# Residual, normalising, modulating and gating of token rows moved from VectorE to GpSimd inside a causal attention stage

## The reference, cut to what matters

```
mod = silu(c) @ wmod                  # sa, ca, ga, sb, cb, gb: six rows of 256 per sequence
ga, gb = clipped away from zero       # |g| >= 0.25
h = layernorm(x) * (1 + ca) + sa
x = x + ga * attention(h)             # 16 heads of 16 features, causal, full softmax
h = layernorm(x) * (1 + cb) + sb      # "h2" below
x = x + gb * ffn(h)                   # 8 experts, each token goes to the best 2
```

## The kernel before, in words

| step | engine | line | chunk number |
|---|---|---|---|
| invert the softmax sums (first block of a sequence) | DVE | L1054 | 32 |
| fetch contexts, inverses and x | POOL queue | L898 to L902 | after the send of the block before |
| normalise the contexts | DVE | L1058 | 50 |
| project | PE | L1212 | 56, 60 |
| gate the attention | DVE | L1064 | 56, 60 |
| residual | DVE | L1072 | 66, 70 |
| statistics, deviation | DVE | L1078, L1086, L1088 | 75, 79 |
| square root | ACT | L947 | six scores behind the deviation's |
| centre and scale | DVE | L1093 | 84 |
| reciprocal, modulate | DVE | L1099, L1105 | 90 |
| transpose h2 | PE | L1221 | 97, 101 |
| router logits | PE | L1229 | 110 |
| choose two experts (compare, order, share) | DVE | L641 to L670 | 120, 123, 126 |
| count and place | PE, then DVE | L678, L691 to L700 | 136 |
| send the rows to their experts' lists | POOL queue | L918 | when placed |
| over | DVE | L1114 | 146 |
| store over | POOL queue | L924 | behind the sends |

## Time and profile before

### The profile page before, as it was taken

One profiled execution on the slowest core, in us unless ns is written; L12 is line 12 of the kernel. 1 busy time (PEld: TensorE's weight loads), 2 busy tenths in 40 slices (PEclk: granted clock), 3 DMA queues, 4 the chain that ended last, 5 costly groups with the idle time before them and its releaser, 6 DMA issues. The chain is left out here.

```text
span 2918.7 us, 49352 instructions
## 1 busy us (share of the span) xinstructions
PE 2574.0 (88%) x16192; PEld 1306.2 (45%) x16192; DVE 2201.2 (75%) x5295; ACT 1734.5 (59%) x3557; POOL 648.1 (22%) x665
## 2 busy tenths in 40 slices
PE   6886899999899999989999998999987569999990
PEld 5771333333333333333333333333332459999990
DVE  6987988888797788878878786888831657777771
ACT  3560277777566666656666665666667137777770
POOL 2224333100010101011010100101011235555663
PEclk8995699999999999999999999999999669999995
DMA  4888778502303214041330404133021635555548
GB/s 144 281 292 272 282 276 294 162 17 64 92 25 98 77 43 114 16 110 40 80 99 25 111 18 108 41 78 101 11 57 46 190 107 90 90 90 90 90 75 245
DMA packets 217119, 331.29 MB, mean 114 GB/s; under 512 B 26736, under 2 KB 157296, under 8 KB 216880
## 3 DMA queue, kind: packets, MB, share of 16 engines
q1 hardware_dynamic: 137728, 170.68, 20.0%
q0 software_dynamic: 58032, 136.67, 18.3%
q10 hardware_dynamic: 21120, 20.97, 2.3%
HBM read 140.23 MB, written 187.20 MB: 112 GB/s over the span
## 5 line engine op out<-in xcount | busy, mean ns | idle before, releaser
L982 ACT ACTIVATE probs<-ps 128x512 f32<-128x512 f32 (+3 forms) x2560 | 1197.5, 539 | 763.9 <-PE ps L1262 383.9
L1006 DVE TENSOR_REDUCE early<-ps 128x1 f32<-128x512 f32 x1536 | 1003.3, 685 | 140.3 <-PE ps L1188 135.5
L1188 PE MATMUL ps<-kh,qs 96*128 96x512 bf16 (+3 forms) x2560 | 904.3, 369 | 114.6 <-DVE early L1006 55.1
L1262 PE MATMUL ps<-qs,kh 99*128 99x512 bf16 (+3 forms) x2560 | 844.7, 355 | 44.1 <-DMA qs<-neg 25.8
L1278 PE MATMUL ps<-probs,vs 128*32 128x512 f32 (+3 forms) x5120 | 612.3, 551 | 0.0
L1188 PEld LDWEIGHTS ps<-kh,qs 96*128 96x128 bf16 x2560 | 252.0, 100 | 751.0 <-DVE early L1006 332.4
L1002 DVE CUSTOM_DVE_ANT_0 junk<-ps,causal 128x128 bf16<-128x128 f32 (+3 forms) x1024 | 481.3, 484 | 68.6 <-PE ps L1188 63.9
L1262 PEld LDWEIGHTS ps<-qs,kh 99*128 99x128 bf16 x2560 | 249.3, 99 | 324.6 <-ACT probs L982 187.0
L918 POOL DMA_INDIRECT rows_out<-row,place_a x96 | 95.5, 995 | 1204.9 <-DVE place_a L700 1159.6
L1677 POOL DMA_INDIRECT acc<-y,to x156 | 250.7, 1607 | 115.8 <-ACT y L1732 70.7
L1266 PE MATMUL ps<-ident_b,causal_b 128*128 128x128 bf16 x1024 | 216.8, 223 | 0.0
(11 more groups left out here) (227 smaller groups left out, 2914.3 us busy)
## 6 DMA issues: line engine op xcount, KB each, us to landing
rows_out<-row POOLq DMA_DIRECT2D x129, 544.0 KB, 3.5
xg<-rows_out SPq DMA_DIRECT2D x39, 544.0 KB
v_ones<-vt SPq DMA_DIRECT2D x16, 1024.0 KB, 6.4
vs<-v_ones SPq DMA_DIRECT2D x16, 1024.0 KB, 7.1
contexts<-ctx_out SPq DMA_DIRECT2D x64, 256.0 KB
q_parts<-parts SPq DMA_DIRECT2D x32, 384.0 KB, 3.8
k_parts<-parts SPq DMA_DIRECT2D x32, 384.0 KB, 4.6
qs<-q_parts SPq DMA_DIRECT2D x64, 192.0 KB, 3.5
```

Of the source, the lines that this page charges most:

```text
L982: nc.scalar.activation(probs[u % PB][:, h, q0:TB], bank(s % SB)[:, q0:TB], ACT.Exp, scale=SCALE).then_inc(exp_done, 1)
L1006: nc.vector.tensor_reduce(early[:, h, t, k0 // CW:k0 // CW + 1], tile, AX.X, ALU.max).then_inc(max_done, 1)
L1188: nc.tensor.matmul(tile[:, 0:w], qh[a % HR][0:STACK, t * P:(t + 1) * P], kh[a % HR][0:STACK, k0:k0 + w], start=True, stop=True).then_inc(m ...
L1262: mm = nc.tensor.matmul(bank(s % SB)[:, q0:TB], kh[a % HR][:, kt * P:(kt + 1) * P], qh[a % HR][:, j * TB + q0:(j + 1) * TB], start=True, s ...
```

## The change

Seven long elementwise operations of each block leave DVE for GpSimd: normalising the contexts (one 128x1024), the two halves of the residual (128x512 each), centring, scaling and modulating, and over (128x1024). DVE did centring and modulating as two times four instructions of 128x256, each with two operations in one; GpSimd does them as four 128x1024 instructions (subtract the mean, times the reciprocal deviation, times the scale row, plus the shift row). GpSimd has no chunk numbers: it takes these steps as soon as their inputs are there, in the order fetch, normalise, token names, residual, residual, modulate, over, store over, send. Before it was fetch, token names, send, store over. What stays on DVE gets new chunk numbers: statistics 69, deviation 73, reciprocal 80; transposes 106 and 110, router 118, choice 128, 131 and 134, count 144. The scores ahead of these are 60 (chunk 69), 63 (73), 70 (80), 126 (144).

```diff
-INVERT, CONTEXT, PROJECT, RESIDUAL, STATISTICS, DEVIATION = 32, 50, (56, 60), (66, 70), 75, 79
-CENTRE, MODULATE, TRANSPOSE, ROUTE, PROBABILITY, RANK = 84, 90, (97, 101), 110, 120, 123
-SHARE, COUNT, OVER = 126, 136, 146
+INVERT, PROJECT, STATISTICS, DEVIATION, SCALE_ROWS = 32, (56, 60), 69, 73, 80
+TRANSPOSE, ROUTE, PROBABILITY, RANK, SHARE, COUNT = (106, 110), 118, 128, 131, 134, 144
...
+                def normalise_contexts(n):
+                    pool.wait_ge(ctx_in, 16 * (2 * KK + 1) * (n + 1))
+                    nc.gpsimd.tensor_tensor(num[:, :, :], num[:, :, :], den[:, :, :], ALU.mult).then_inc(ctx_norm, 1)
+
+                def residual(n, half):
+                    pool.wait_ge(gated_done, 2 * n + half + 1)
+                    ts = slice(2 * half, 2 * half + 2)
+                    nc.gpsimd.tensor_tensor(xres[:, ts, :], gated[:, ts, :], xres[:, ts, :], ALU.add
+                                            ).then_inc(res_done, 1)
...
+                def modulate(n):
+                    rows, wide = [P, TT, D], centred[:, :, :]
+
+                    def linked(step, ins):
+                        ins.then_inc(centred_done, 1)
+                        pool.wait_ge(centred_done, 3 * n + step)
+
+                    pool.wait_ge(var_done, (2 * TT + 1) * (n + 1))
+                    pool.wait_ge(o_mm, 2 * (n + 1))
+                    linked(1, nc.gpsimd.tensor_tensor(wide, xres[:, :, :], mv[:, :, 0:1].to_broadcast(rows), ALU.subtract))
+                    pool.wait_ge(rstd_done, n + 1)
+                    linked(2, nc.gpsimd.tensor_tensor(wide, wide, rstd[:, :].unsqueeze(2).to_broadcast(rows), ALU.mult))
+                    linked(3, nc.gpsimd.tensor_tensor(
+                        wide, wide, keep.mod_rows[:, n // BPB, 1, :].unsqueeze(1).to_broadcast(rows), ALU.mult))
+                    nc.gpsimd.tensor_tensor(row[:, :, 0:D], wide,
+                                            keep.mod_rows[:, n // BPB, 0, :].unsqueeze(1).to_broadcast(rows),
+                                            ALU.add).then_inc(h2_done, 1)
...
                     fetch(n)
+                    normalise_contexts(n)
                     name_tokens(n)
+                    for half in range(2):
+                        residual(n, half)
+                    modulate(n)
+                    over_gate(n)
+                    store_over(n)
                     send(n)
-                    store_over(n)
...
-                def modulate(n):
+                def scale_rows(n):
                     dve.wait_ge(rooted, n + 1)
                     nc.vector.reciprocal(rstd[:, :], rstd[:, :]).then_inc(rstd_done, 1)
```

More of the change, by code:

```diff
@@ L903, in fetch, with over_gate @@
                                         ).then_inc(ctx_in, 16)
+                def normalise_contexts(n):
[6 more added lines that the diff above has]
+                                            ).then_inc(res_done, 1)
+                def over_gate(n):
+                    if n == 0:
+                        pool.wait_ge(mod_steps, 2 + 2 * B)
+                    pool.wait_ge(res_done, 2 * (n + 1))
+                    pool.wait_ge(ctx_norm, n + 1)
+                    nc.gpsimd.tensor_tensor(over[:, :, :], xres[:, :, :],
+                                            keep.gate_inv[:, n // BPB, :].unsqueeze(1).to_broadcast([P, TT, D]),
+                                            ALU.mult).then_inc(over_done, 1)
+                def modulate(n):
[13 more added lines that the diff above has]
+                                            ALU.add).then_inc(h2_done, 1)
                 def name_tokens(n):
@@ L1067, in gate_attention @@
                                             ALU.mult).then_inc(gated_done, 1)
[L1069 to L1073, removed]
                 def statistics(n):
@@ L1082, in deviation @@
                     if n:
[L1083 removed]
+                        dve.wait_ge(h2_done, n)
                     for t in range(TT):
@@ L1088, in deviation @@
                     nc.vector.tensor_scalar(rstd[:, :], mv[:, :, 1], EPS, None, ALU.add).then_inc(var_done, 1)
[L1090 to L1095, removed]
-                def modulate(n):
+                def scale_rows(n):
                     dve.wait_ge(rooted, n + 1)
                     nc.vector.reciprocal(rstd[:, :], rstd[:, :]).then_inc(rstd_done, 1)
-                    dve.wait_ge(rstd_done, n + 1)
-                    if n:
-                        dve.wait_ge(sent, 128 * n)
-                    for t in range(TT):
-                        dve.wait_ge(centred_done, TT * n + t + 1)
-                        nc.vector.scalar_tensor_tensor(out=row[:, t, 0:D], in0=centred[:, t, :],
-                                                       scalar=rstd[:, t:t + 1], in1=keep.mod_rows[:, n // BPB, 0, :],
-                                                       op0=ALU.mult, op1=ALU.add).then_inc(h2_done, 1)
-                def over_gate(n):
-                    if n == 0:
-                        dve.wait_ge(mod_steps, 2 + 2 * B)
-                    dve.wait_ge(ctx_norm, n + 1)
-                    dve.wait_ge(res_done, 2 * (n + 1))
-                    nc.vector.tensor_tensor(over[:, :, :], xres[:, :, :],
-                                            keep.gate_inv[:, n // BPB, :].unsqueeze(1).to_broadcast([P, TT, D]),
-                                            ALU.mult).then_inc(over_done, 1)
                 def count(n):
@@ L1139, in _ @@
                                 invert(n // BPB)
-                            if c == CONTEXT:
-                                normalise_contexts(n)
                             if c in PROJECT:
                                 gate_attention(n, PROJECT.index(c))
-                            if c in RESIDUAL:
-                                residual(n, RESIDUAL.index(c))
                             if c == STATISTICS:
@@ L1159, in _ @@
                             if c == SHARE:
+                                if n:
+                                    dve.wait_ge(sent, 128 * n)
                                 choice.share(nc, dve, n, RS, r_steps, row)
```

17 lines of the change are left out of this document (5 added, 12 removed).

## The result

| | before | after |
|---|---|---|
| median, us (20 runs each) | 2920.9 | 2937.1 |
| from, to | 2907.7, 2937.8 | 2927.3, 2945.2 |
| profiled execution's span | 2918.7 | 2934.0 |
| granted clock, mean | 0.929 | 0.928 |

The ratio is 1.0047, 95% interval 1.0034 to 1.006: the change made the kernel **slower by 0.5%**, about 16 us, where 40 us less was forecast; the range of the forecast was 2858 to 2912 us.

The account below looks back on a forecast made before the run. PE bounds block-free streams; a routing block adds 22.5 us, eleven times, partly through DVE. Terms -43 - 5.5 - 9 + 7 + 10 = -40.5 us from 2920.5 gave 2880 us, range 2858 to 2912.

Parts of the forecast that it names:

- DVE's bursts and over: Around chunks 66 to 97, PE regains 3.9 of 4.3 us a block (-43); over at chunk 146 gives -5.5 us.
- the root: At the reciprocal DVE stands about 1.2 us for ACT's root; PE loses 0.6 us a block, +7 us in all.
- The choice: Choice of experts at chunks 128, 131, 134 has more scores between its pieces; 0.8 us a block off, -9 us.
- The fetch: At the turn, fetch starts 1.2 us nearer, delaying stores of maxima; 1.3 us in each of eight groups, +10 us.
- rival 3: GpSimd's products hold up DVE's chunk work through the shared port: +47.5 us, 2968 us; chance 0.05.
- Rival 2: Around chunks 66 to 97 PE itself is the limit, so only visible waits go: -5 us, 2915 us; chance 0.10.
- Rival 1: At the turn, fetch delays maxima stores more, with low clock after: +56 instead of +10, 2926 us; chance 0.07.
- The streams: Expected sign: attention streams with a routing block go from 126.5 to about 123 us.
- the distance: Expected sign: time between two p_v batches around chunks 66 to 97 falls from 25.5 to near 20.3 us.
- the waits for `qs<-neg`: Expected sign: PE's waits for stores of the negated maxima come near 30 us instead of 22.6.
- four signs of being wrong: Longer chunk lines, PE waiting for GpSimd, `qs<-neg` waits above 50 us, or p_v batch distance staying near 25 us.

Follow-up runs that it names:

- b_fetchwait: The kernel before, with the fetch of contexts held until the stores of the negated maxima have landed, so the two cannot collide; 2878.3 us, ratio 0.9841.
- a_oldnum: The changed kernel with the old chunk numbers for transposes (97/101), router (110), choice (120/123/126) and count (136); 2857.5 us, ratio 0.9793.
- a_count144_fw: The changed kernel with old chunk numbers except count at 144, and the fetch held until the stores of the negated maxima have landed; 2866.1 us, ratio 0.983.
- a_choice128_fw: The changed kernel with only transposes and router at old chunks, and the fetch held until the stores of the negated maxima have landed; 2878.8 us, ratio 0.9861.
- a_fetchwait: The changed kernel, new chunk numbers kept, with the fetch held until the stores of the negated maxima have landed; 2880.4 us, ratio 0.9872.
- a_count144: The changed kernel with the old chunk numbers except count at 144, fetch not held; 2928.3 us, ratio 1.0019.
- a_choice128: The changed kernel with only transposes and router at their old chunks (choice 128/131/134, count 144), fetch not held; 2930.4 us, ratio 1.003.
- a_old_newton2: The changed kernel with old chunk numbers and the inverse root without ACT: first value from the variance's bits on DVE, three GpSimd steps; 2842.9 us, ratio 0.9737.
- b_newnum: The kernel before with only the new chunk numbers for transposes, router, choice and count, long operations still on DVE; 2937.4 us, ratio 1.0086.

## Why the prediction was wrong

The runs give the whole way from one kernel to the other, each step the difference of two runs:

| step | from, to | us by the medians | us by the ratios |
|---|---|---|---|
| take the collision out of the kernel before | before, b_fetchwait | -42.6 | -46 |
| move the operations to GpSimd | b_fetchwait, a_oldnum | -20.8 | -14 |
| count at 144 | a_oldnum, a_count144_fw | +8.6 | +11 |
| choice at 128 to 134 | a_count144_fw, a_choice128_fw | +12.7 | +9 |
| transposes, router later | a_choice128_fw, a_fetchwait | +1.6 | +3 |
| put the collision back | a_fetchwait, after | +56.7 | +51 |
| sum | before, after | +16.2 | +14 |

The last column takes each step from the two ratios to the kernel before, times 2921 us. The columns differ by up to 7 us, so no step is known better than that, and one of 2 us is none; the signs of the large ones are the same in both. The second step takes the hold away too, which a_oldnum does not need: there the store of over no longer stands ahead of the fetch. The text below uses the medians.

The forecast was -40.5 and the result +16.2. The 56.7 us between them (by chance the same number as the collision's) are: 20.7 in moving the operations, 21.7 in the choice, 8.6 in the count, 1.6 in transposes and router, 4.1 in the fetch.

- **DVE's bursts and over (-43 and -5.5) with the root (+7): -41.5 predicted, -20.8 measured.** The bursts' part was nearly right: without the root batches 18 to 25 go from 61.7 to 25.3, 36 us against 43, and the batch at over from 6.4 to 0, against 5.5. The term that was mis-sized is the root: +7 predicted, +23.7 measured. I priced DVE's wait for it, 1.2 us estimated and 0.58 measured, which turned out to cost nothing, and not ACT itself: 2.8 us a block in which no exponential is made, which cost nothing before and **23.7 us** now. The table load stands in the earlier trace rows; I read it as a delay for DVE only.
- **The choice (-9): +12.7, and the count, which had no term: +8.6.** This step failed, and with its sign. I argued that the new chunks have more scores between the pieces. That PE runs dry twice there all the same, for some 8 us over the streams, and what the clock may do then, I did not ask, though the earlier trace rows shows such a fall behind another wait. The later count I carried into the fetch alone.
- **The fetch (+10): 56.7 - 42.6 = +14.1.** Mechanism and place were right, and the size about right (by the ratios it is +5): the start moved by 0.6 us in most turns (1.2 predicted), PE's waits for the stores rose by 11.7 us. Some of the nearness is luck: by the table 12.5 us of the 56.7 lie in batches 30 to 39, not at the turn. But the sum treats as an increment what is really two large terms, 43 us of loss that were already in the kernel before and need not be there. I had its sign in the earlier trace rows, 6.6 against 2.2 us, and never asked what the whole would be worth.
- **Not happened: GpSimd disturbing DVE** (rival 3). Chunk maxima of 512 columns take 685 ns and reductions 686, before 686 and 685, as the rule has it that the prediction cites from the Trainium skill, "SBUF — State Buffer", Who interferes with whom. No product is late: PE waits nowhere for GpSimd. Rival 2 is out as well: with the old numbers and without the root the same move gives 2833.8 us, and batches 18 to 25 lose 36 us less. Rival 1 named the collision and comes nearest in time (2926), but for the wrong reason: it expected 46 us more of the collision than the forecast, and it was 4.
- **The signs named beforehand.** The streams take 127.9 us on the mean, not 123; the distance is 22.5, not 20.3; the waits for `qs<-neg` are 34.3, near the 30 expected. None of the four signs of being wrong came: the chunk lines are no longer, PE does not wait for GpSimd, the waits are under 50, the distance is not near 25. None of them watched the choice, where the sum counted a gain, or the count, which had no term.

What stays open: with the collision the choice's place costs nothing (2928.3 and 2930.4), without it 12.7. In the profiled executions of a_count144 and a_choice128 the clock costs 75.2 and 63.2 us by the slices, more in the first, so the clock there offsets what the choice adds in waiting. Why it does so was not tried.

The move is worth making, the later chunk numbers that came with it are not: a_oldnum is 2.1% below the kernel before, and a_old_newton2, which adds the root without ACT, 2.6%. Most of the 2.1% is not DVE's relief, though: holding the fetch alone takes 1.6% off the kernel before.

## What to carry to other kernels

When work leaves the limiting engine, price what lay hidden under it on every other engine, an isolated ACT function with its table loads above all. A large transfer issued in the background can hold up a small store on which PE waits, and when it starts decides: mostly 3.0 us ahead of the turn PE waited 22.6 us in all, 2.4 us ahead 34.3, some 6 us ahead 2.2. Ask where a queue's head stands against the small stores, whether or not the change means to touch it. Try a change of schedule numbers apart from the change of code that it came with.

## What the runs showed of the hardware

- A GpSimd product whose second operand is one number repeated along the row is faster than one with a full row, where I had allowed up to twice as slow. Groups of instructions, after:

```profile
L935 POOL TENSOR_TENSOR work<-work,mod_rows 128x1024 f32<-128x1024 f32 x12 | 28.4, 2363 | 0.9
...
L934 POOL TENSOR_TENSOR work<-work,rstd_b 128x1024 f32<-128x1024 f32 x12 | 22.7, 1894 | 40.1 <-DVE rstd_b L1123 40.1
```

- How long a 16 KB store takes to land goes by when the 1.5 MB fetch began. In the three turns looked at above it is 2.2 us with the fetch 6.1 us ahead of the turn, 7.5 with it 2.4 ahead, and 2.3 with it 5 us behind. Other turns of a_oldnum, with the fetch 5.3 to 6.4 us ahead, have up to 4.1. In b_newnum, where the fetch began 2.0 us behind the turn at 1524.1, the first two stores land in 2.2 us and the third in 5.8.
- A wait of PE can cost it more than the wait. In the kernel after PE waits 3.3 to 5.1 us at each of the eight turns with a collision at the head of a stream, and behind each its clock is at the lower of its two levels for 3.4 or 6.8 us, 17 us in all by the slices (an estimate), beside 30 us of waiting. In the kernel before, with waits of 1.4 to 3.1 us, this is so behind six of the eight.
